# Row groups' small VectorE operations on one column each, and GpSimd's byte operations in eight pieces of 256 columns

## The chip, the cores and the metric

The kernel runs on one core of a Trainium2 chip. The metric is the device time of one execution in microseconds (us).

## The reference

Two batches of 1024 tokens with 2048 features go through a quantized product and then through a dense layer with routed low-rank additions:

```
q1 = fake_quant(layernorm(x), x1_scale, x1_zp)     # clip(round(v / s + z), 0, 255), (q - z) * s
q2 = fake_quant(ctx_4096, x2_scale, x2_zp)
x  = x + q1 @ q2                                   # (2, 1024, 2048) @ (2, 2048, 2048)
y  = layernorm(x)
w  = top-2 of softmax(y @ W_router.T), normalized, over 8 experts
x  = x + y @ W_base.T + b_base + 2 * sum_e w_e * (y @ lora_A[e].T) @ lora_B[e].T
```

## The kernel before

The kernel is written engine by engine: each engine has its own program in a fixed order, and semaphores tie them together. Nothing is scheduled at run time, so the order of work on an engine is the order of its code.

Only the first product concerns us. A "row" is a tile of 128 tokens by 2048 features; there are 8 for each batch, numbered T = 0 to 15. For each row VectorE (DVE) takes statistics (`ln_stats_of`: four `bn_stats`, one `bn_aggr`, and, at the last row of a group, two small operations L950 and L951 that put variance + eps and minus the mean in the small tile `lnt`). Rows go in groups of one or two (`LN_GROUPS`: rows 0, 1, 2, 3-4, 5-6, 7, 8-9, ...). ScalarE (ACT) takes the square root (`ln_std_of`), and `ln_scale_of` on DVE makes from it, with one Newton step, a scale (column 4 of `lnt`) and an offset (column 5) for each row of the group. With these, either ACT (`ln_bytes_of`) or GpSimd (POOL, `row_bytes_of`, for rows 2, 4, 6 and 9) turns the row into bytes. TensorE (PE) turns the bytes (`turn(T)`, L1700), ACT copies them out of PSUM (`ln_copy`, L724), and they are the moving side of the first product.

The other side, the context, comes in 32 columns n of 128 x 2048 values, 1 MB each. POOL turns each to bytes (`ctx_bytes_of`, L1611), and ACT (L733) or DVE (`ctx_ready_of`, L1005) makes them float16. PE works in chunks (`chunk(n, c)`, 16 matmuls, L1721) into a ring of four PSUM banks; DVE frees a bank with `take_y(n, c)` (L1022), which adds the chunk to x. Behind it come ACT's column addition and high part (`col_add_of`, `hi_of`, L747), DVE's low part (`lo_of`, L1028) and the sum of squares (`acc_of`, L1041). SyncE (SP) issues all loads from one queue in order; a context load waits for POOL to be done with the buffer's former column.

POOL's own order is: small constants, then context bytes 0, row 2, context 1, row 4, context 2, row 6, context 3, context 4, row 9, context 5 and so on. PE's order up to the first full stretch is: `turn(0)`, `turn(1)`, `turn(2)`, `chunk(0,0)`, `turn(3)`, `turn(4)`, `chunk(1,0)`, `chunk(0,1)`, `chunk(1,1)`, `chunk(2,0)`, `turn(5)`, `turn(6)`, `chunk(2,1)`, `chunk(0,2)`, `turn(7)`, `chunk(1,2)`, `chunk(2,2)`, with short sums between them.

Of the kernel before, what the change touches and what calls it, by code (L numbers as in the profile page):

```python
# [8 lines left out]
ALU = mybir.AluOpType  # L9
# [9 lines left out]
CH = 512  # L19
# [83 lines left out]
def xattn_ffn(nc, x, xT, ctx, s1, z1, s2, z2, w_t, w_n, bias, ar, b_t, outT):  # L103

    es = ExitStack()
    with es:
# [120 lines left out]
        def pc(i):  # L227
            return par[:, i:i + 1]

        S1, Z1, S2, Z2 = pc(0), pc(1), pc(2), pc(3)  # L230
        IS1, IS2, C1, C2, D1, D2 = pc(4), pc(5), pc(6), pc(7), pc(8), pc(9)
        RC1, RC2, LO1, HI1, LO2, HI2 = pc(10), pc(11), pc(12), pc(13), pc(14), pc(15)
        S12, ND1S, ND2S, DDS, YB = pc(16), pc(17), pc(18), pc(19), pc(20)
# [694 lines left out]
        def _(dve):  # L928
            V = nc.vector

            def ln_stats_of(T):
# [17 lines left out]
                dve.wait_ge(ln_stat, 2 * T + 2)  # L949
                V.tensor_scalar(lnt[g % 2][:, 0, 0:w], mv[:, t0:t0 + w, 1], EPS, None, ALU.add)  # L950
                V.tensor_scalar(lnt[g % 2][:, 6, 0:w], mv[:, t0:t0 + w, 0], -1.0, None, ALU.mult).then_inc(ln_var, 1)  # L951

            def ln_scale_of(g):


                t0, w = LN_GROUPS[g]
                n = lnt[g % 2]
                dve.wait_ge(ln_std, g + 1)
                V.reciprocal(n[:, 1, 0:w], std1[:, t0:t0 + w]).then_inc(ln_newton, 1)
                dve.wait_ge(ln_var, g + 1)  # L960
                dve.wait_ge(ln_newton, 4 * g + 1)
                for m in range(w):
                    ins = V.scalar_tensor_tensor(n[:, 2, m:m + 1], n[:, 1, m:m + 1], n[:, 0, m:m + 1], n[:, 1, m:m + 1], ALU.mult, ALU.mult)
                ins.then_inc(ln_newton, 1)
                dve.wait_ge(ln_newton, 4 * g + 2)
                V.tensor_scalar(n[:, 2, 0:w], n[:, 2, 0:w], -0.5, 1.5, ALU.mult, ALU.add).then_inc(ln_newton, 1)
                dve.wait_ge(ln_newton, 4 * g + 3)
                V.scalar_tensor_tensor(n[:, 4, 0:w], n[:, 2, 0:w], IS1, n[:, 1, 0:w], ALU.mult, ALU.mult).then_inc(ln_newton, 1)
                dve.wait_ge(ln_newton, 4 * g + 4)
                for m in range(w):  # L970
                    ins = V.scalar_tensor_tensor(n[:, 5, m:m + 1], n[:, 4, m:m + 1], n[:, 6, m:m + 1], Z1, ALU.mult, ALU.add)
                ins.then_inc(ln_scale, 1)
# [618 lines left out]
        def _(pool):  # L1591
# [398 lines left out]
```

## Time and profile before

| | |
|---|---|
| median of 3 runs | 987.72 us (987.59 to 987.99) |
| the profiled execution | 987.62 us, span 985.9 us |
| PE busy | 958.5 us (97% of the span), 5829 matmuls |
| DVE busy | 791.3 us (80%) |
| ACT busy | 429.3 us (44%) |
| POOL busy | 150.3 us (15%), 204 instructions |
| moved by DMA | 185.65 MB |

Times in the trace are from the start of the span. The execution's own time is 1.7 us longer than its span. A busy share is a mean over stages: PE's 97% says that the 27 us in which it is not busy are what a change outside PE can reach, and the views by stage show where they lie.

### The profile page before, as it was taken

What the parts mean: (1) busy time and instruction counts of PE and PEld (TensorE: products, weight loads), DVE (VectorE), ACT (ScalarE), POOL (GpSimd) and SP (SyncE); (2) the same over time, 40 slices, a digit from 0 to 9 for tenths busy, and PEclk for the clock granted to TensorE, in tenths of its full rate; (3) what the DMA queues carried; (4) which work ended last, traced back from release to release, by engine and by line L of the source; (5) the groups of instructions that cost most, each with busy time, mean ns of one, the idle gap of its engine ahead of it and who ended that gap; (6) DMA issues with size and microseconds to landing.
All of it is one profiled execution on the core that took longest, in us unless ns stands there. A gap on an engine that the chain in (4) does not pass through costs nothing.

```text
span 985.9 us, 15054 instructions
## 1 busy us (share of the span) xinstructions
PE 958.5 (97%) x5829; PEld 525.2 (53%) x5829; DVE 791.3 (80%) x1427; ACT 429.3 (44%) x466; POOL 150.3 (15%) x204
## 2 busy tenths in 40 slices
PE   2899999999999999999999999999999999999998
PEld 1776666666799444444444444444444444444444
DVE  7998988989636878997876887757879788798786
ACT  4888887565532444554444542212232323323310
POOL 5655435455000000000000000000000000000000
PEclk9999999999999999999999999999999999999999
DMA  9977776987434337866674674178533143242220
GB/s 375 372 263 296 261 295 236 324 310 254 142 116 143 126 81 251 268 191 242 226 232 161 200 249 103 40 238 283 170 114 127 61 144 128 71 154 93 85 75 33
DMA packets 62311, 185.65 MB, mean 188 GB/s; under 512 B 6896, under 2 KB 19488, under 8 KB 56096
## 3 DMA queue, kind: packets, MB, share of 16 engines
q1 hardware_dynamic: 58648, 174.18, 49.7%
q0 software_dynamic: 1280, 2.12, 2.4%
q10 hardware_dynamic: 2312, 8.39, 2.2%
q8 instruction: 46, 0.75, 0.3%
q14 instruction: 25, 0.20, 0.1%
HBM read 151.07 MB, written 33.60 MB: 187 GB/s over the span
## 4 chain that ended last, share of the span: by engine, by line
PE 92%; DVE 0%; issue 0%
PE pair L1884 34%; PE pair L1908 29%; PE pair L1721 19%; PE pair L1846 5%; PE pair L1856 4%; PE pair L1920 1%; PE pair L1729 0%; PE pair L1700 0%; PE pair L1826 0%; PE pair L1741 0%; DVE xt L1022 0%; DVE sq L1536 0%; DVE u L1538 0%; PE pair L1735 0%; PE pair L1745 0%
## 5 line engine op out<-in xcount | busy, mean ns | idle before, releaser
L1884 PE MATMUL pair<-x2p,w_p 128*128 128x512 f16 x1536 | 337.0, 379 | 0.0
L1884 PEld LDWEIGHTS pair<-x2p,w_p 128*128 128x128 f16 x1536 | 150.3, 98 | 180.4
L1721 PE MATMUL pair<-q1T,ctx_q 128*128 128x342 f16 (+2 forms) x1584 | 228.3, 304 | 1.8 <-DVE xt L1022 1.7
L1721 PEld LDWEIGHTS pair<-q1T,ctx_q 128*128 128x128 f16 x1584 | 152.7, 97 | 72.0 <-issue 2.8
L1908 PE MATMUL pair<-x2p,w_slot 128*128 128x512 f16 x744 | 163.8, 379 | 0.0
L841 ACT ACTIVATE sq<-pair,lsc 128x512 f32<-128x512 f32 x64 | 43.5, 681 | 210.0 <-PE pair L1856 174.1
L1611 POOL TENSOR_SCALAR ctx_u<-ctx_f,par 128x512 uint8<-128x512 f32 x128 | 113.5, 901 | 96.6 <-DMA ctx_f<-in_ctx 79.7
L1908 PEld LDWEIGHTS pair<-x2p,w_slot 128*128 128x128 f16 x744 | 72.9, 98 | 87.7
L869 ACT ACTIVATE w_slot<-w_q,usc 128x1024 f16<-128x1024 f32 x32 | 36.5, 1146 | 91.9 <-DVE usc L1442 27.2
L1908 PE MATMUL pair<-x2p,x2p 128*128 128x512 f16 x336 | 74.3, 379 | 0.0
L739 ACT ACTIVATE xt<-xt,colt 128x1024 f32<-128x1024 f32 x32 | 36.7, 1146 | 54.8 <-DVE xt L1022 54.8
L1466 DVE SCALAR_TENSOR_TENSOR w_slot<-w_q,usc,w_slot 128x1024 f16<-128x1024 f32 x32 | 40.6, 1282 | 22.8 <-ACT w_slot L869 22.8
L1028 DVE SCALAR_TENSOR_TENSOR x2p<-xt,xs,x2p 128x1024 f16<-128x1024 f32 x32 | 42.4, 1327 | 17.4 <-ACT x2p L747 17.2
L1022 DVE SCALAR_TENSOR_TENSOR xt<-pair,par,xt 128x342 f32<-128x342 f32 (+2 forms) x99 | 53.9, 552 | 2.9 <-PE pair L1721 2.1
L869 ACT ACTIVATE x2p<-w_q,usc 128x1024 f16<-128x1024 f32 x24 | 27.4, 1146 | 65.9 <-DVE usc L1442 15.8
L825 ACT ACTIVATE w_p<-w_f,wsc 128x1024 f16<-128x1024 f32 x32 | 34.9, 1138 | 48.7 <-DVE wsc L1211 48.7
L1908 PEld LDWEIGHTS pair<-x2p,x2p 128*128 128x128 f16 x336 | 32.8, 98 | 39.7
L1908 PE MATMUL pair<-x2p 128*128 128x512 f16 x240 | 52.9, 379 | 0.0
L1856 PE MATMUL pair<-hwT,b_p 128*128 128x512 f16 x192 | 51.7, 379 | 0.0
L1672 POOL DMA_DIRECT2D scratch<-w_max x16 | 9.0, 559 | 279.8 <-DVE w_max L1200 261.5
L1411 DVE SCALAR_TENSOR_TENSOR u<-sq,bias_s,u 128x512 f32<-128x512 f32 x63 | 47.4, 752 | 2.2
L1846 PE MATMUL pair<-ar_p,x2p 128*128 128x137 f16 x768 | 48.3, 224 | 0.0
(217 smaller groups left out, 1110.0 us busy)
## 6 DMA issues: line engine op xcount, KB each, us to landing
ctx_f<-in_ctx SPq DMA_DIRECT2D x32, 1024.0 KB, 7.6
xt<-in_xT SPq DMA_DIRECT2D x32, 512.0 KB, 4.7
w_r<-in_w_n SPq DMA_DIRECT2D x32, 512.0 KB, 7.0
w_f<-in_w_t SPq DMA_DIRECT2D x32, 512.0 KB, 5.9
w_q<-in_w_t SPq DMA_DIRECT2D x32, 512.0 KB, 4.9
outT<-u SPq DMA_DIRECT2D x63, 256.0 KB, 3.2
rows<-in_x SPq DMA_DIRECT2D x15, 1024.0 KB, 9.7
x_kept<-xt ACTq DMA_DIRECT2D x16, 512.0 KB, 4.3
```

What stands on the lines that cost most here:

```text
L841: A.activation(sq[m % 2][:, :], lora_bank(m)[:, :], ACT.Copy, scale=by).then_inc(lora_taken, 1)
L869: A.activation(w_of(i, p, 0), w_q[s][:, :, :], ACT.Copy, scale=usc[:, i % 2, (3 if by == 4 else 2):(4 if by == 4 else 3)]).then_inc(s_hi, 1)
L1022: V.scalar_tensor_tensor(xt[n % 3][:, t], bank[at % RING][:, 0:w], S12, xt[n % 3][:, t], ALU.mult, ALU.add).then_inc(y_taken, 1)
L1028: V.scalar_tensor_tensor(x2p[b][:, j, 1, :], xt[n % 3][:, :], xs[:, b, 0:1], x2p[b][:, j, 0, :], ALU.mult, ALU.subtract).then_inc(lo_done, 1)
L1411: V.scalar_tensor_tensor(o[:, :], s[:, :], bias_s[:, j:j + 1], o[:, :], ALU.add, ALU.add).then_inc(u_ready, 1)
L1466: V.scalar_tensor_tensor(w_of(i, p, 1), w_q[s][:, :, :], usc[:, i % 2, (3 if by == 4 else 2):(4 if by == 4 else 3)], w_of(i, p, 0), ALU.mu ...
L1611: ins = G.tensor_scalar(ctx_u[n % 2][:, c], ctx_f[n % 2][:, c], IS2, Z2, ALU.mult, ALU.add)
L1721: ins = M.matmul(bank[at % RING][:, 0:w], ctx_q[n % NQ][:, k, :], q1T[b][:, k, t0:t0 + w], start=(k == 0), stop=(k == KT - 1))
L1846: ins = M.matmul(h_tile(b, t), x2p[b][:, k, xh, t * P:(t + 1) * P], ar_p[ah][:, k, :], start=(k == 0 and q == 0), stop=(k == KT - 1 and q ...
L1856: ins = M.matmul(lora_bank(m)[:, :], b_p[s][bh][:, :], hwT[b][hh][:, t], start=(q == 0), stop=(q == 2))
L1884: M.matmul(base_bank(m)[:, :], w_p[j % 2][wh][:, k, :], x2p[0][:, k, xh, t], start=(k == 0 and q == 0), stop=(k == KT - 1 and q == 2))
L1908: ins = M.matmul(product_bank(i, p)[:, :], w_of(i, p, wh)[:, k // 4, (k % 4) * P:(k % 4 + 1) * P], x_of(p, k, xh), start=(k == 0 and q == ...
```

## The change

In the row groups, each small operation that had two columns for a group of two rows becomes two operations of one column. The three kinds of `scalar_tensor_tensor`, which read two tensors of `lnt`, become `tensor_scalar` operations of one column, whose other operands are given as scalars of the partition. The algebra is reordered for it: (v r r - 3) times (-r / (2 S1)) in place of (1.5 - 0.5 v r r) times IS1 times r, so that `NIS1` takes the place of `IS1`, and a chain of four dependent steps behind the reciprocal becomes one of three. On POOL each burst of four operations of 512 columns becomes one of eight operations of 256.

```diff
-                V.tensor_scalar(lnt[g % 2][:, 0, 0:w], mv[:, t0:t0 + w, 1], EPS, None, ALU.add)
-                V.tensor_scalar(lnt[g % 2][:, 6, 0:w], mv[:, t0:t0 + w, 0], -1.0, None, ALU.mult).then_inc(ln_var, 1)
+                for m in range(w):
+                    V.tensor_scalar(lnt[g % 2][:, 0, m:m + 1], mv[:, t0 + m, 1:2], EPS, None, ALU.add)
+                for m in range(w):
+                    ins = V.tensor_scalar(lnt[g % 2][:, 6, m:m + 1], mv[:, t0 + m, 0:1], -1.0, None, ALU.mult)
+                ins.then_inc(ln_var, 1)
...
                 V.reciprocal(n[:, 1, 0:w], std1[:, t0:t0 + w]).then_inc(ln_newton, 1)
                 dve.wait_ge(ln_var, g + 1)
-                dve.wait_ge(ln_newton, 4 * g + 1)
+                dve.wait_ge(ln_newton, 3 * g + 1)
                 for m in range(w):
-                    ins = V.scalar_tensor_tensor(n[:, 2, m:m + 1], n[:, 1, m:m + 1], n[:, 0, m:m + 1], n[:, 1, m:m + 1], ALU.mult, ALU.mult)
+                    V.tensor_scalar(n[:, 2, m:m + 1], n[:, 0, m:m + 1], n[:, 1, m:m + 1], n[:, 1, m:m + 1], ALU.mult, ALU.mult)
+                for m in range(w):
+                    ins = V.tensor_scalar(n[:, 3, m:m + 1], n[:, 1, m:m + 1], NIS1, None, ALU.mult)
                 ins.then_inc(ln_newton, 1)
-                dve.wait_ge(ln_newton, 4 * g + 2)
-                V.tensor_scalar(n[:, 2, 0:w], n[:, 2, 0:w], -0.5, 1.5, ALU.mult, ALU.add).then_inc(ln_newton, 1)
-                dve.wait_ge(ln_newton, 4 * g + 3)
-                V.scalar_tensor_tensor(n[:, 4, 0:w], n[:, 2, 0:w], IS1, n[:, 1, 0:w], ALU.mult, ALU.mult).then_inc(ln_newton, 1)
-                dve.wait_ge(ln_newton, 4 * g + 4)
+                dve.wait_ge(ln_newton, 3 * g + 2)
                 for m in range(w):
-                    ins = V.scalar_tensor_tensor(n[:, 5, m:m + 1], n[:, 4, m:m + 1], n[:, 6, m:m + 1], Z1, ALU.mult, ALU.add)
+                    ins = V.tensor_scalar(n[:, 4, m:m + 1], n[:, 2, m:m + 1], 3.0, n[:, 3, m:m + 1], ALU.subtract, ALU.mult)
+                ins.then_inc(ln_newton, 1)
+                dve.wait_ge(ln_newton, 3 * g + 3)
+                for m in range(w):
+                    ins = V.tensor_scalar(n[:, 5, m:m + 1], n[:, 4, m:m + 1], n[:, 6, m:m + 1], Z1, ALU.mult, ALU.add)
                 ins.then_inc(ln_scale, 1)
...
             dve.wait_ge(par_turned, 1)
+            V.tensor_scalar(S1N, bank[0][:, 0:1], -2.0, None, ALU.mult)
             V.tensor_copy(par[:, 0:4], bank[0][:, 0:4]).then_inc(par_copied, 1)
             dve.wait_ge(par_copied, 1)
-            V.reciprocal(IS1, S1)
+            V.reciprocal(NIS1, S1N)
...
-                for q in range(4):
-                    c = slice(q * CH, (q + 1) * CH)
+                for q in range(8):
+                    c = slice(q * CH // 2, (q + 1) * CH // 2)
                     ins = G.tensor_scalar(ctx_u[n % 2][:, c], ctx_f[n % 2][:, c], IS2, Z2, ALU.mult, ALU.add)
...
-                for q in range(4):
-                    c = slice(2 * q, 2 * q + 2)
+                for q in range(8):
+                    c = slice(q, q + 1)
                     ins = G.tensor_scalar(byte[:, c, :, :], row[:, c, :, :], lnt[g % 2][:, 4, m:m + 1], lnt[g % 2][:, 5, m:m + 1], ALU.mult, ALU.add)
```

On DVE, around the group of rows 5 and 6 (`lnt_146`), the program stood so before; `xt` rows are `take_y`, the `ctx_q` row is `ctx_ready_of(2)`, and `rows_0_53` is row 7:

```order
L950 TENSOR_SCALAR lnt_146<-mv 128x2
L951 TENSOR_SCALAR lnt_146<-mv 128x2
L1022 SCALAR_TENSOR_TENSOR xt_79<-pair,par,xt_79 128x256
L959 RECIPROCAL lnt_146<-std_145 128x2
L963 SCALAR_TENSOR_TENSOR lnt_146<-lnt_146 128x1 x2
L966 TENSOR_SCALAR lnt_146<-lnt_146 128x2
L968 SCALAR_TENSOR_TENSOR lnt_146<-lnt_146,par 128x2
L971 SCALAR_TENSOR_TENSOR lnt_146<-lnt_146,par 128x1 x2
L1005 TENSOR_SCALAR ctx_q_78<-ctx_u_74,par 128x2048
L1022 SCALAR_TENSOR_TENSOR xt_80<-pair,par,xt_80 128x256
L1022 SCALAR_TENSOR_TENSOR xt_79<-pair,par,xt_79 128x256
L940 BN_STATS stats_143<-rows_0_53 128x6 x4
```

and stands so now (the line numbers are those of the changed kernel, 1 to 8 higher):

```order
L952 TENSOR_SCALAR lnt_146<-mv 128x1 x2
L954 TENSOR_SCALAR lnt_146<-mv 128x1 x2
L1029 SCALAR_TENSOR_TENSOR xt_79<-pair,par,xt_79 128x256
L964 RECIPROCAL lnt_146<-std_145 128x2
L968 TENSOR_SCALAR lnt_146<-lnt_146 128x1 x2
L970 TENSOR_SCALAR lnt_146<-lnt_146,par 128x1 x2
L974 TENSOR_SCALAR lnt_146<-lnt_146 128x1 x2
L978 TENSOR_SCALAR lnt_146<-lnt_146,par 128x1 x2
L1012 TENSOR_SCALAR ctx_q_78<-ctx_u_74,par 128x2048
L1029 SCALAR_TENSOR_TENSOR xt_80<-pair,par,xt_80 128x256
L1029 SCALAR_TENSOR_TENSOR xt_79<-pair,par,xt_79 128x256
L941 BN_STATS stats_143<-rows_0_53 128x6 x4
```

Nothing changes its place; nine small instructions of the group become thirteen, and none of them reads two tensors or has two columns any more, the reciprocal aside.

On POOL, the bursts from context column 0 to context column 3 stood so before:

```order
L1611 TENSOR_SCALAR ctx_u_74<-ctx_f_72,par 128x512 x4
L1625 TENSOR_SCALAR q1u_0_62<-rows_2_55,lnt_146 128x2x2x128 x4
L1611 TENSOR_SCALAR ctx_u_75<-ctx_f_73,par 128x512 x4
L1625 TENSOR_SCALAR q1u_0_62<-rows_4_57,lnt_147 128x2x2x128 x4
L1611 TENSOR_SCALAR ctx_u_74<-ctx_f_72,par 128x512 x4
L1625 TENSOR_SCALAR q1u_0_62<-rows_6_59,lnt_146 128x2x2x128 x4
L1611 TENSOR_SCALAR ctx_u_75<-ctx_f_73,par 128x512 x4
```

and stand so now:

```order
L1619 TENSOR_SCALAR ctx_u_74<-ctx_f_72,par 128x256 x8
L1633 TENSOR_SCALAR q1u_0_62<-rows_2_55,lnt_146 128x2x128 x8
L1619 TENSOR_SCALAR ctx_u_75<-ctx_f_73,par 128x256 x8
L1633 TENSOR_SCALAR q1u_0_62<-rows_4_57,lnt_147 128x2x128 x8
L1619 TENSOR_SCALAR ctx_u_74<-ctx_f_72,par 128x256 x8
L1633 TENSOR_SCALAR q1u_0_62<-rows_6_59,lnt_146 128x2x128 x8
L1619 TENSOR_SCALAR ctx_u_75<-ctx_f_73,par 128x256 x8
```

The order is the same, each burst has twice the instructions, and its semaphore still rises only behind the last of them.

## Rows read from the trace of the kernel before

**Rows 1.** Busy time by stage: window, its length, each engine, PEclk, DMA share, GB/s

```profile
20.00:40.00 20.00, 15.95 (x191) 13.56 (x192) 18.70 (x46) 14.81 (x10) 15.92 (x21) 1.00 1.02 418
...
60.00:80.00 20.00, 18.27 (x131) 11.97 (x129) 19.31 (x36) 17.63 (x15) 11.46 (x13) 1.00 0.81 302
...
100.00:985.90 885.90, 882.37 (x5104) 467.53 (x5101) 703.51 (x1226) 354.35 (x410) 90.59 (x113) 1.00 0.51 173
```

**Rows 2.** What PE waited for from 44 to 90 us: total, times, longest

```profile
PE pair L1721 <- DVE xt L1022: 1.7, 2, 1.0
```

**Rows 3.** Timeline, 72 to 80.7 us: start, us, instructions, idle before and releaser

```profile
73.29 0.44 DVE L950 TENSOR_SCALAR lnt<-mv 128x2 f32<-128x2 f32 x1
...
74.44 0.79 DVE L963 SCALAR_TENSOR_TENSOR lnt<-lnt 128x1 f32<-128x1 f32 x2
...
77.19 0.57 DVE L1022 SCALAR_TENSOR_TENSOR xt<-pair,par,xt 128x342 f32<-128x342 f32 x1
...
77.90 2.48 PE L1721 MATMUL pair<-q1T,ctx_q 128*128 128x342 f16 x16 [1.01 <-DVE xt L1022]
```

**Rows 4.** Timelines of ACT and of DVE, 43 to 100 us

```profile
52.66 2.10 ACT L716 ACTIVATE q1u<-rows,lnt 128x2048 uint8<-128x2048 f32 x1 [1.85 <-DVE lnt L971]
...
67.09 1.67 DVE L1028 SCALAR_TENSOR_TENSOR x2p<-xt,xs,x2p 128x1024 f16<-128x1024 f32 x1 [0.31 <-ACT x2p L747]
```

**Rows 5.** Timeline of DVE, 32.9 to 44.9 us

```profile
33.62 0.48 DVE L1022 SCALAR_TENSOR_TENSOR xt<-pair,par,xt 128x256 f32<-128x256 f32 x1 [0.50 <-DMA xt<-in_xT]
...
34.28 0.35 DVE L963 SCALAR_TENSOR_TENSOR lnt<-lnt 128x1 f32<-128x1 f32 x2
...
35.39 1.28 DVE L1005 TENSOR_SCALAR ctx_q<-ctx_u,par 128x2048 f16<-128x2048 uint8 x1
...
40.27 0.15 DVE L950 TENSOR_SCALAR lnt<-mv 128x1 f32<-128x1 f32 x1
40.34 0.14 DVE L951 TENSOR_SCALAR lnt<-mv 128x1 f32<-128x1 f32 x1
...
41.06 0.78 DVE L963 SCALAR_TENSOR_TENSOR lnt<-lnt 128x1 f32<-128x1 f32 x1
41.88 0.15 DVE L966 TENSOR_SCALAR lnt<-lnt 128x1 f32<-128x1 f32 x1
42.07 0.52 DVE L968 SCALAR_TENSOR_TENSOR lnt<-lnt,par 128x1 f32<-128x1 f32 x1
...
42.75 1.07 DVE L1022 SCALAR_TENSOR_TENSOR xt<-pair,par,xt 128x256 f32<-128x256 f32 x2
```

**Rows 6.** Timeline of POOL, 18 to 44 us

```profile
19.41 3.03 POOL L1625 TENSOR_SCALAR q1u<-rows,lnt 128x512 uint8<-128x512 f32 x4 [2.32 <-DVE lnt L971]
...
35.57 4.00 POOL L1625 TENSOR_SCALAR q1u<-rows,lnt 128x512 uint8<-128x512 f32 x4 [2.53 <-DVE lnt L971]
39.55 3.03 POOL L1611 TENSOR_SCALAR ctx_u<-ctx_f,par 128x512 uint8<-128x512 f32 x4
```

**Rows 7.** Timeline of POOL, 11 to 13.9 us, its small constants

```profile
11.23 0.29 POOL L1649 TENSOR_SCALAR par<-par 128x1 f32<-128x1 f32 x1
11.49 0.28 POOL L1650 TENSOR_SCALAR par<-par 128x1 f32<-128x1 f32 x1
```

**Rows 8.** Timeline of PE, 38 to 110 us

```profile
39.63 0.62 PE L1700 MATMUL pair<-ident,q1w 128*128 128x128 f16 x8 [0.53 <-POOL q1u L1625]
...
40.49 1.91 PE L1721 MATMUL pair<-q1T,ctx_q 128*128 128x256 f16 x16
...
46.21 0.62 PE L1700 MATMUL pair<-ident,q1w 128*128 128x128 f16 x8 [1.07 <-ACT q1u L716]
```

**Rows 9.** Timeline of DVE, 9.8 to 20 us

```profile
14.23 0.60 DVE L968 SCALAR_TENSOR_TENSOR lnt<-lnt,par 128x1 f32<-128x1 f32 x1
...
18.40 0.22 DVE L963 SCALAR_TENSOR_TENSOR lnt<-lnt 128x1 f32<-128x1 f32 x1
18.65 0.15 DVE L966 TENSOR_SCALAR lnt<-lnt 128x1 f32<-128x1 f32 x1
```

**Rows 10.** What the trace has of POOL's `ctx_u` instructions: ns min/median/max, starts

```profile
L1611 POOL TENSOR_SCALAR ctx_u<-ctx_f,par x128: 767/772/2775, 14.1 to 246.9; 128x512 uint8<-128x512 f32 x128
```

More of the change, by code:

```diff
@@ L230, in xattn_ffn @@
         S1, Z1, S2, Z2 = pc(0), pc(1), pc(2), pc(3)
-        IS1, IS2, C1, C2, D1, D2 = pc(4), pc(5), pc(6), pc(7), pc(8), pc(9)
-        RC1, RC2, LO1, HI1, LO2, HI2 = pc(10), pc(11), pc(12), pc(13), pc(14), pc(15)
+        NIS1, IS2, C1, C2, D1, D2 = pc(4), pc(5), pc(6), pc(7), pc(8), pc(9)
+        S1N, LO1, LO2 = pc(10), pc(12), pc(14)
         S12, ND1S, ND2S, DDS, YB = pc(16), pc(17), pc(18), pc(19), pc(20)
```

## The prediction

> **What bounds the kernel now.** I read the page first: PE is busy 97% of the span. Then the busy time by stage, for where the other 27 us lie [rows 1]: from 20 to 40 us PE works 15.95 us, from 60 to 80 it works 18.27, and from 100 us to the end 882.37 of 885.90. The list of waits names no wait of PE behind 90 us. So what the change can move is the moment at which PE becomes gapless, 77.90 us, and nothing later, as long as POOL's longer bursts keep up.
>
> From 44 us on PE has three waits: 1.07 us before `turn(7)` at 46.21 [rows 8], and 1.7 us in two waits for DVE to free a bank [rows 2], the last of which ends with `chunk(5,2)` at 77.90, released by DVE's take at 77.19 [rows 3]. That bounds a gain: even a DVE that is never late gives at most 1.7 + 1.1 = 2.8 us.
>
> I follow that take back. DVE is busy 19.31 of the 20 us from 60 to 80 [rows 1], with one stop, 0.31 us before the low part at 67.09, for ACT's high part [rows 4]. ACT in turn works without a stop from 52.66, when the scale of rows 8-9 lets it start that row's bytes [rows 4], having waited 1.85 us for it. So the path is: DVE's `ln_scale_of(6)` at 52.6, ACT until 67.06, DVE until 77.76, PE. Before 52.6 DVE has no stop back to 33.62, where it waits 0.50 us for the first x tile's DMA [rows 5], in a stage in which the DMA engines are full (share 1.02) [rows 1]. What DVE gains before 33.62 waits there for the same load and is lost.
>
> **The stalls.** The small operations show a price alone and a price beside POOL. A two-tensor operation of one column takes 0.22 us when POOL is idle (18.40) [rows 9], and 0.60, 0.78 and 0.52 us when a burst runs [rows 9, 5]. The 0.78 at 41.06 begins with a POOL piece (39.55 plus two pieces of 0.76), and lasts just one piece [rows 5, 6]. Between the two blocked ones stands a `tensor_scalar` of one column, 0.15 us, with POOL just as busy [rows 5]: one column and one tensor isn't blocked. The same with two columns is: L950 takes 0.44 at 73.29 [rows 3], against 0.15 for one column [rows 5].
>
> The Trainium skill (SBUF — State Buffer, The single rule) says it the same way: an exclusive lock on a port pair, held for a whole instruction, between GpSimd and VectorE operations with two SBUF inputs or in a 2-port mode. By that rule the one-column `tensor_scalar` never waits; the trace agrees with its 0.15 us.
>
> **The change part by part.**
>
> (a) DVE on the path, saved. Group of row 7: L963 0.78 and L968 0.52 fall to some 0.22 each [rows 5, 9], 0.56 + 0.30 = 0.86 us. Group of rows 10-11: L950 0.44 to 0.15, 0.29 us; L963's pair takes 0.79 [rows 3] against 0.35 for such a pair with POOL idle [rows 5], 0.44 us. In sum 0.73 us behind 67.09 and 0.86 before 42.6. The stalls before 33.62 (0.38 at 14.23 [rows 9], and others like it) are worth nothing, by the wait for the load.
>
> (b) DVE on the path, added. A dependent step costs about 0.25 us from start to start (18.40 to 18.65) [rows 9] or 0.19 (41.88 to 42.07), and an independent instruction behind another 0.07 (L950 to L951) to 0.13 (the second of a pair, 0.35 less 0.22) [rows 5]. For a group of one row one step of 0.19 goes and one of 0.1 comes: 0.1 less. For a group of two, the step with four instructions costs 0.64 in place of 0.38, the next 0.38 in place of 0.20, and one step of 0.26 goes: 0.18 more; L950 and L951 become four, 0.14 more. What a `tensor_scalar` of one column with two pointers costs is in no row; between the 0.15 of one without [rows 5] and the 0.22 of the operation that it replaces [rows 9] I take 0.22; at 0.15 it would be some 0.1 less for each group. On the path there are the groups of rows 5-6 (+0.18), 7 (-0.1), 8-9 (+0.32) and 10-11 (+0.32). The instruction `S1N` (+0.07, at 9 us) is hidden by the same load.
>
> (c) POOL. No piece of 256 columns is in the trace. From below: it costs half of a piece of 512, 0.385 us, and a burst stays 3.03. From above: it costs as much as a piece of 512, 0.77, and a burst takes 6.1. Between them I take the middle between one column with a pointer (0.29 long, 0.26 from 11.23 to the next start) [rows 7] and 512 columns (0.76 to the next) [rows 6], the two rows on either side: 0.51 us, a burst of 4.07, 1.04 more. The Trainium skill (GPSIMD Engine Reference, Elementwise — side-by-side cycle accounting) gives 1.8 cycles an element at 1.2 GHz, and predicts 768 ns for 512 elements from it with no fixed part; by it 256 would take 384 ns and nothing would be added. The row of 0.29 us for one column speaks against that.
>
> (d) What POOL's microsecond does. Before, POOL stood idle 2.32 and 2.53 us for DVE's scales ahead of rows 2 and 6 [rows 6]; the second is what takes up the longer bursts. Row 2 starts at 18.95 (19.41 less 0.38 and 0.1), and row 2, context 1, row 4 and context 2 then run on end: 18.95 + 4 x 4.07 = 35.23, where context 2 ended at 35.57 - 2.53 = 33.04 before [rows 6]. DVE wants context 2 at 35.39 + 0.18 = 35.57 [rows 5]: just in time. Row 6 starts behind it, and loses the 1.0 us that it lost before (4.00 against 3.03) to the same DVE operation of 1.28 us [rows 5, 6]: it ends at 35.57 + 0.18 + 1.0 + 4.07 = 40.8 in place of 39.57. `turn(6)` waits for it now as before (0.53 us at 39.63) [rows 8], so `chunk(2,1)` (40.49 + 1.91 = 42.40) [rows 8] ends at 42.40 + 1.25 = 43.65. DVE wants that chunk for the second of its takes at 42.75, which began near 43.2 [rows 5]. DVE itself would be there at 43.2 + 0.18 - 0.1 - 0.86 = 42.4, waits until 43.7, and is 0.5 us later than before. So the 0.86 us of the row-7 group is eaten whole.
>
> Queued behind that take are `bound`, the statistics of rows 8 and 9, and `ln_scale_of(6)`: ACT's start at 52.66 moves by 0.5 + 0.32 = 0.8 us. `turn(7)` depends on ACT's copies behind the standard deviation of row 7 and moves by 0.2. ACT's stretch keeps its length, and DVE's own work in it, which had 0.31 us to spare and meets POOL in pieces half as long, stays hidden. Of the 0.8 at 67.09, the change then takes off 0.73 (a), adds 0.32 (b), and the low part there, long at 1.67 us beside a burst [rows 4], is held on average for half a piece, 0.25 in place of 0.38: 0.13 less. The sum is 0.8 - 0.73 + 0.32 - 0.13 = +0.26 us. PE's gaps of 1.7 us [rows 2] only shift with it.
>
> (e) Later POOL bursts. A column takes PE 48 matmuls of 342 columns, about 7 us; POOL needs 3.03 of them, or 4.0 where it meets DVE, and then 5.1. The trace names no engine that waited for these instructions [rows 10]. POOL mostly waits for the context load, and the loads are started by the x tile's place in the same queue rather than by POOL. SP's queue: contexts 2, 3 and 4 are issued 1 to 2 us later, each while the DMA engines are full with what was issued ahead of them (share 1.02) [rows 1], so the bytes land as before; context 5 goes out behind context 3's burst (39.55 + 3.03 = 42.58) [rows 6], some 2.3 us later, and POOL wants it behind row 9, whose bytes wait for the scale of 52.66 [rows 4], ten microseconds on. I cost (e) at nothing; if the cover were gone, it would be up to 1 us for each column.
>
> The sum against the profiled execution is 987.62 + 0.26 = 987.88; the median of the runs is 0.1 above that execution, so 988.0 us.
>
> **The rivals.**
> - *Slower: POOL's bursts become the path.* Place: context 2 and row 6, at 35 to 41 us. From a burst b above 4.15 us, DVE's L1005 at 35.57 has to wait, and row 6 ends at about 20.15 + 5b; each 0.1 us on a burst costs 0.5. At +2 us in all, b is about 4.45, a piece 0.556 us. At 0.60 a piece it gives 987.9 + 5 x 0.73 = 991.5 or so, at the upper bound of 0.77 some 998. For it: a fixed cost could lie above the 0.26 of one column, since the byte operations have two pointers and another output type. Against it: the 0.29 at 11.23 [rows 7] is with a pointer too. Chance 0.09.
> - *Faster: the relief gets through.* If a piece costs 0.385, row 6 ends 0.1 later, the chunk is there, and DVE is 0.76 early at the second take; ACT starts 0.4 earlier, and with the 0.56 behind 67.09 the take at 77.19 comes 0.95 earlier: 986.8. This is the case in which the page's rate holds. Chance 0.13. PE's two waits of 1.7 us [rows 2] are all that it can use, unless `turn(7)` comes earlier too.
> - *The change doesn't free DVE:* a pointer operand may be held back like a tensor. No row shows a pointer with an SBUF input beside a running burst. The stalls in (a) then last half a piece less, and 67.09 on saves 0.4 rather than 0.73: +0.6, 988.3. Chance 0.05.
>
> **How the numbers follow.** The likeliest case (0.73) is the sum with a piece between 0.47 and 0.54 us: 987.6 to 988.8. A measurement tells 0.2%, about 2 us, from no change, so faster means below 985.7 and slower above 989.7. Faster takes 0.02, out of the second rival. Slower takes 0.09, nearly all of the first rival and a little of the others. The rest, 0.89, is the same. The range from 986.7 to 989.6 takes in the likeliest case, the rest of the second and third rivals, and the start of the first, and leaves out the rest of it.
>
> **What the new profile would show.** A POOL piece of 256 columns at 0.51 us; row 6's burst ending near 40.8; DVE stopped about 1.3 us before the second take of column 2, for PE; no one-column operation on `lnt` over 0.25 us; ACT's bytes of row 8 at about 53.5; PE's last gap ending near 78.2. The prediction is wrong if a piece costs over 0.55 us, or if the stop at 33.62 goes, since then DVE's early savings count.

## The result, and the profile after

The changed kernel takes 992.38 us (median of 6 runs, 990.52 to 993.58) beside 987.84 us of the kernel before (6 runs, 987.58 to 988.50): a ratio of 1.0043, 95% interval 1.0034 to 1.0053. It is 4.5 us slower, where 988.0 was forecast, with a range of 986.7 to 989.6. The profiled execution took 991.65 us, its span is 989.8 us against 985.9 before: 3.9 us more to find. Lines from the diff on have moved by 1 to 8: L1022, L1028, L1611, L1625, L1700, L1721 of before are L1029, L1035, L1619, L1633, L1708, L1729 here.

The busy time from 20 to 40 us, columns as in [rows 1] (PE, its weight loads, DVE, ACT, POOL), and then a part of that stretch in steps of 2 us:

```profile
20.00:40.00 20.00, 14.84 (x160) 12.73 (x161) 17.20 (x51) 14.70 (x10) 20.00 (x37) 0.91 1.02 417
```
```profile
30.00:32.00 2.00, 0.19 (x4) 0.10 (x3) 1.97 (x4) 2.00 (x2) 2.00 (x5) 0.95 0.99 397
32.00:34.00 2.00, 2.00 (x18) 1.89 (x19) 0.74 (x6) 1.84 (x3) 2.00 (x5) 0.50 1.07 438
34.00:36.00 2.00, 2.00 (x15) 1.58 (x13) 1.69 (x10) 1.04 (x2) 2.00 (x4) 0.70 0.97 397
```

POOL, busy for 15.92 us of the stretch from 20 to 40 before [rows 1], is busy for all 20 of it. And behind a PE that worked 0.19 us from 30 to 32 us the granted clock stands at 0.50 (of its two levels, 1.2 in place of 2.4 GHz) from 32 to 34 us, and at 0.70 in the mean from 34 to 36, a stretch in which it rises again; before, the whole stretch had 1.00 [rows 1].

POOL's timeline, against [rows 6]:

```profile
18.99 4.30 POOL L1633 TENSOR_SCALAR q1u<-rows,lnt 128x256 uint8<-128x256 f32 x8 [0.60 <-DVE lnt L978]
23.27 4.30 POOL L1619 TENSOR_SCALAR ctx_u<-ctx_f,par 128x256 uint8<-128x256 f32 x8
27.55 4.30 POOL L1633 TENSOR_SCALAR q1u<-rows,lnt 128x256 uint8<-128x256 f32 x8
31.83 4.30 POOL L1619 TENSOR_SCALAR ctx_u<-ctx_f,par 128x256 uint8<-128x256 f32 x8
36.11 5.27 POOL L1633 TENSOR_SCALAR q1u<-rows,lnt 128x256 uint8<-128x256 f32 x8
```

A burst takes 4.30 us, 1.27 more than the 3.03 of before, 8 pieces of 0.535 us from start to start. These five bursts stand end to end; of the 2.32 and 2.53 us for which POOL waited for DVE before [rows 6], 0.60 is left. Row 4's bytes (27.55) end at 31.85, 1.8 us later than before, and row 6's (36.11) at 41.38.

PE's timeline, against [rows 3, 8]:

```profile
31.91 1.03 PE L1708 MATMUL pair<-ident,q1w 128*128 128x128 f16 x8 [1.81 <-POOL q1u L1633]
33.59 2.70 PE L1729 MATMUL pair<-q1T,ctx_q 128*128 128x256 f16 x16
36.53 5.40 PE L1729 MATMUL pair<-q1T,ctx_q 128*128 128x256 f16 x48
43.07 1.91 PE L1729 MATMUL pair<-q1T,ctx_q 128*128 128x256 f16 x16
...
79.89 2.48 PE L1729 MATMUL pair<-q1T,ctx_q 128*128 128x342 f16 x16 [1.17 <-DVE xt L1029]
...
109.30 2.48 PE L1729 MATMUL pair<-q1T,ctx_q 128*128 128x342 f16 x16 [0.47 <-DVE xt L1029]
...
121.89 4.81 PE L1729 MATMUL pair<-q1T,ctx_q 128*128 128x342 f16 x32 [0.36 <-DVE xt L1029]
...
139.70 2.48 PE L1729 MATMUL pair<-q1T,ctx_q 128*128 128x342 f16 x16 [0.93 <-DVE xt L1029]
```

The 3.9 us stand here in two halves. The last early gap ends at 79.89, not 77.90 [rows 3]: 2.0. And behind 100 us, where the list of before had no wait of PE, there are three for DVE's take: 0.47 + 0.36 + 0.93 = 1.76. That leaves some 0.15. The windows show the same: from 120 to 140 us PE works 18.71 us, where it worked 19.90 before, and from 140 to 250 all of it in both.

Between those two halves, DVE and ACT, against [rows 4, 5]:

```profile
33.65 0.48 DVE L1029 SCALAR_TENSOR_TENSOR xt<-pair,par,xt 128x256 f32<-128x256 f32 x1 [1.15 <-DMA xt<-in_xT]
...
42.58 0.27 DVE L968 TENSOR_SCALAR lnt<-lnt 128x1 f32<-128x1 f32 x1
...
45.01 0.48 DVE L1029 SCALAR_TENSOR_TENSOR xt<-pair,par,xt 128x256 f32<-128x256 f32 x1 [1.09 <-PE pair L1729]
```
```profile
54.91 2.10 ACT L717 ACTIVATE q1u<-rows,lnt 128x2048 uint8<-128x2048 f32 x1 [2.30 <-DVE lnt L978]
```

DVE gains 0.65 us before 33.65 and gives it to the x tile's load (its stop is 1.15 where it was 0.50). The row-7 group is no longer held (0.27 where 0.78 stood), and the second take of column 2 then waits 1.09 us for PE. ACT starts row 8's bytes at 54.91, 2.25 us late.

What the trace has of the small operations on `lnt`, over all groups (ns, min/median/max):

```profile
L968 DVE TENSOR_SCALAR lnt<-lnt x16: 262/272/275, 9.2 to 136.5; 128x1 f32<-128x1 f32 x16
L970 DVE TENSOR_SCALAR lnt<-lnt,par x16: 202/204/206, 9.4 to 136.8; 128x1 f32<-128x1 f32 x16
L974 DVE TENSOR_SCALAR lnt<-lnt x16: 204/214/215, 9.7 to 137.2; 128x1 f32<-128x1 f32 x16
L978 DVE TENSOR_SCALAR lnt<-lnt,par x16: 262/272/275, 9.9 to 137.6; 128x1 f32<-128x1 f32 x16
```

The longest of 16 is 3 ns above the median: no one-column `tensor_scalar` is ever held, with one pointer (an operand given as one value for each partition) or two. But one with two pointers takes 0.27 us, not the 0.22 of the operation that it replaced.

### The profile page after: what moved, and what is told of

It reads as the page before. It is cut to its first block, busy times and chain, and to the rows that moved or that the text cites. A ratio compares the mean times of both kernels' runs of the same rounds, so it can differ in the third digit from the quotient of the medians.

```text
span 989.8 us, 15223 instructions
## 1 busy us (share of the span) xinstructions
PE 960.1 (97%) x5829; PEld 526.7 (53%) x5829; DVE 790.6 (80%) x1452; ACT 429.1 (43%) x466; POOL 219.0 (22%) x348
## 4 chain that ended last, share of the span: by engine, by line
PE 86%; DVE 0%; issue 0%
PE pair L1892 33%; PE pair L1916 29%; PE pair L1729 13%; PE pair L1854 5%; PE pair L1864 4%; PE pair L1928 1%; PE pair L1737 0%; PE pair L1834 0%; PE pair L1708 0%; PE pair L1749 0%; DVE sq L1544 0%; DVE xt L1029 0%; DVE u L1546 0%; PE pair L1743 0%; PE pair L1828 0%; PE pair L1841 0%
## 5 line engine op out<-in xcount | busy, mean ns | idle before, releaser
L1729 PE MATMUL pair<-q1T,ctx_q 128*128 128x342 f16 (+2 forms) x1584 | 229.6, 305 | 3.4 <-DVE xt L1029 3.4
L1729 PEld LDWEIGHTS pair<-q1T,ctx_q 128*128 128x128 f16 x1584 | 153.1, 98 | 74.3 <-issue 5.2
L1619 POOL TENSOR_SCALAR ctx_u<-ctx_f,par 128x256 uint8<-128x256 f32 x256 | 176.1, 702 | 40.9 <-DMA ctx_f<-in_ctx 30.4
L1029 DVE SCALAR_TENSOR_TENSOR xt<-pair,par,xt 128x342 f32<-128x342 f32 (+2 forms) x99 | 53.9, 551 | 5.1 <-PE pair L1729 3.5
L1035 DVE SCALAR_TENSOR_TENSOR x2p<-xt,xs,x2p 128x1024 f16<-128x1024 f32 x32 | 43.0, 1344 | 18.1 <-ACT x2p L748 17.8
L1916 PEld LDWEIGHTS pair<-x2p,x2p 128*128 128x128 f16 x336 | 32.9, 98 | 39.7
```

The lines of the kernel that those rows point to most:

```text
L1029: V.scalar_tensor_tensor(xt[n % 3][:, t], bank[at % RING][:, 0:w], S12, xt[n % 3][:, t], ALU.mult, ALU.add).then_inc(y_taken, 1)
L1035: V.scalar_tensor_tensor(x2p[b][:, j, 1, :], xt[n % 3][:, :], xs[:, b, 0:1], x2p[b][:, j, 0, :], ALU.mult, ALU.subtract).then_inc(lo_done, 1)
L1729: ins = M.matmul(bank[at % RING][:, 0:w], ctx_q[n % NQ][:, k, :], q1T[b][:, k, t0:t0 + w], start=(k == 0), stop=(k == KT - 1))
L1916: ins = M.matmul(product_bank(i, p)[:, :], w_of(i, p, wh)[:, k // 4, (k % 4) * P:(k % 4 + 1) * P], x_of(p, k, xh), start=(k == 0 and q == ...
```

## The experiments

Theory P (POOL's longer bursts make the loss) and theory G (DVE's longer groups) stood against each other first, and within P whether the loss is made early (before 45 us) or late (behind 80). No kernel leaves out work that the reference asks for; each ratio is to the kernel before, run beside it.

**One part alone.** From the kernel before, only POOL's two loops:

```
-                for q in range(4):
-                    c = slice(q * CH, (q + 1) * CH)
+                for q in range(8):
+                    c = slice(q * CH // 2, (q + 1) * CH // 2)
...
-                for q in range(4):
-                    c = slice(2 * q, 2 * q + 2)
+                for q in range(8):
+                    c = slice(q, q + 1)
```

> The kernel before with GpSimd's bursts in eight pieces of 256 columns and nothing else. Theory P (the bursts do it): bursts of 4.30 us in place of 3.03 delay row 4, row 6 and the context loads by themselves; 990 to 993 us, last early gap of PE ending 2 us or more later than 77.90, new waits of PE for VectorE behind 100 us. Theory G (the longer groups of two on VectorE do a good half): this kernel takes half of the loss or less, 988.5 to 990, and PE has no new wait behind 100 us.

Measured: 990.99 us (990.11 to 993.53, 5 runs), ratio 1.0034 [1.0022, 1.0047], +3.1. P holds for the larger part. PE waits for POOL twice before 45 us:

```profile
32.36 0.62 PE L1700 MATMUL pair<-ident,q1w 128*128 128x128 f16 x8 [1.65 <-POOL q1u L1625]
...
42.41 0.62 PE L1700 MATMUL pair<-ident,q1w 128*128 128x128 f16 x8 [1.14 <-POOL q1u L1625]
```

With the groups of before, row 6 ends at 42.35 (its burst starts at 37.08), later than the 41.38 of the changed kernel: there the groups' new form does help POOL, by 1.0 us. The last early gap ends at 80.54, and one late wait of 0.47 is left. The clock stays at 1.00 in this kernel.

The other part alone: the changed kernel with both loops back at four pieces of 512.

> The changed kernel with GpSimd's bursts back at four pieces of 512; VectorE's one-column operations stay. Theory P: no slower than before, and up to 1 us faster, since the 0.94 us of stalls at 41 to 42.6 us now reach the take of column 2: 986.8 to 988.0. Theory G: the groups of two are 0.4 us longer each, the loads of rows behind them come later, and PE gets waits behind 100 us: 989 to 990.5.

Measured: 988.60 us (988.15 to 988.96, 11 runs), ratio 1.0005 [0.9996, 1.0013]. The whole program's relief of DVE is worth nothing, or less; the loss of 0.66 us on the median isn't told from zero, since the interval holds 1. DVE and POOL around the row-7 group:

```profile
41.38 0.27 DVE L968 TENSOR_SCALAR lnt<-lnt 128x1 f32<-128x1 f32 x1
...
39.85 3.01 POOL L1619 TENSOR_SCALAR ctx_u<-ctx_f,par 128x512 uint8<-128x512 f32 x4
```
```profile
77.45 2.48 PE L1729 MATMUL pair<-q1T,ctx_q 128*128 128x342 f16 x16 [1.05 <-DVE xt L1029]
118.95 4.81 PE L1729 MATMUL pair<-q1T,ctx_q 128*128 128x342 f16 x32 [0.27 <-DVE xt L1029]
136.80 2.48 PE L1729 MATMUL pair<-q1T,ctx_q 128*128 128x342 f16 x16 [0.93 <-DVE xt L1029]
```

At 41.38 a two-pointer operation runs its plain 0.27 us inside a burst of 512-column pieces: the rival "the change doesn't free DVE" falls. PE's last early gap ends 0.45 us earlier than before, and 1.20 us of late waits take it back: 0.75 more in all, and 0.66 measured on the median.

**The clock.** The changed kernel with filler matmuls, so that PE isn't idle ahead of row 4:

```
             turn(3)
+            keep_busy(26)
             turn(4)
```

> The changed kernel with 26 filler matmuls between turn(3) and turn(4), in the 1.8 us in which PE waits for row 4's bytes and behind which its granted clock falls to 0.50. Theory C (the fall of the clock is a part of the first 2 us): chunk(1,0) takes 1.9 us again in place of 2.70, PE is about 1.5 us ahead at chunk(2,1), the second take of column 2 comes about 1 us earlier, and the time is 0.5 to 1.5 us under the changed kernel's 992.4. Rival (VectorE and ScalarE are late anyway by the bursts): the clock stays at 1.0 and the time stays within 0.3 us of the changed kernel.

Measured: 993.50 us (993.49 to 995.33, 5 runs), ratio 1.0057 [1.0044, 1.0070]; 1.1 us above the changed kernel, which neither theory had. The stretch behind row 4, and PE's waits, from `turn(6)` on:

```profile
32.00:34.00 2.00, 2.00 (x31) 1.89 (x29) 0.65 (x6) 2.00 (x3) 2.00 (x4) 1.00 1.04 426
```
```profile
41.48 0.62 PE L1708 MATMUL pair<-ident,q1w 128*128 128x128 f16 x8 [0.50 <-POOL q1u L1633]
...
79.10 2.48 PE L1729 MATMUL pair<-q1T,ctx_q 128*128 128x342 f16 x16 [0.93 <-DVE xt L1029]
106.45 2.48 PE L1729 MATMUL pair<-q1T,ctx_q 128*128 128x342 f16 x16 [0.74 <-DVE xt L1029]
109.87 2.48 PE L1729 MATMUL pair<-q1T,ctx_q 128*128 128x342 f16 x16 [0.93 <-DVE xt L1029]
123.75 4.81 PE L1729 MATMUL pair<-q1T,ctx_q 128*128 128x342 f16 x32 [1.66 <-DVE xt L1029]
141.54 0.74 PE L1729 MATMUL pair<-q1T,ctx_q 128*128 128x342 f16 x4 [0.92 <-DVE xt L1029]
```

The clock is whole again and the last early gap ends 0.8 us earlier (79.10, not 79.89). It isn't kept: the late waits grow from 1.76 to 4.25 us. So undoing the fall of the clock doesn't bring the time back, and an earlier start into the late stage buys nothing here. What the fall costs by itself isn't shown, since this kernel's late part differs too. One thing the first line adds: with a whole clock PE waits for row 6's bytes at `turn(6)` again, 0.50 us, though row 4's are as late as ever, and `chunk(2,1)` starts at 42.34.

**Late bursts in eight, early in four**, with DVE's new form:

```
+                parts = 8 if n >= 4 else 4
+                for q in range(parts):
+                    c = slice(q * D // parts, (q + 1) * D // parts)
```

(and in the rows' loop the same with `T >= TT`).

> The changed kernel with the bursts of rows 2, 4, 6 and of context columns 0 to 3 back at four pieces of 512; those of columns 4 on and of row 9 stay at eight of 256. If the first 2 us (PE's last early gap ends at 79.9 in place of 77.9) come from the early bursts alone and the other 2 us (waits of PE from 109 to 140 us) from the late ones: 989.5 to 990.5, gap at 78, and the late waits stay. If the late waits only follow from the early lateness: 987.5 to 988.5.

Measured: 990.18 us (988.62 to 991.79, 11 runs), ratio 1.0021 [1.0012, 1.0030]. The last early gap ends at 77.54, earlier than before, and the late waits are 0.93 + 0.33 + 0.93 = 2.2 us. So there is a late loss with an undisturbed early part: 1.6 us of time, and 1.0 us of late waits, more than in the kernel with DVE's new form alone.

**Larger pieces.** From the kernel before, two pieces of 1024 columns in a burst in place of four of 512.

> The kernel before with GpSimd's bursts in two pieces of 1024 columns and nothing else. By a straight line through what was measured (0.535 us a piece of 256, 0.757 a piece of 512) a piece has a fixed 0.31 us and 0.87 us for 1000 columns: 1.20 us for 1024, a burst of 2.40 in place of 3.03. Theory P (the length of the bursts sets the time): no slower than before, 986.5 to 987.9. Rival (what counts is how long one piece holds VectorE): held operations wait up to 1.2 us, VectorE is later at the takes at 43 and 77 us, and the time is 988.5 or more.

Measured: 989.12 us (988.65 to 990.30, 11 runs), ratio 1.0012 [1.0003, 1.0021]. What the trace has of `ctx_u`, and, in the profiled execution (the slowest of the 11), two of PE's waits:

```profile
L1611 POOL TENSOR_SCALAR ctx_u<-ctx_f,par x64: 1184/1195/3062, 14.1 to 246.9; 128x1024 uint8<-128x1024 f32 x64
```
```profile
77.69 2.48 PE L1721 MATMUL pair<-q1T,ctx_q 128*128 128x342 f16 x16 [1.91 <-DVE xt L1022]
80.73 1.47 PE L1721 MATMUL pair<-q1T,ctx_q 128*128 128x342 f16 x9 [0.56 <-DVE xt L1022]
```

A burst is 2.37 us, 0.66 shorter, and the kernel is slower all the same: PE waits 4.2 us for takes from 69 to 81, where it waited 1.7 [rows 2]. What is held on DVE can now be held for most of a piece of 1.19 us (L951 takes 1.03 us at 76.05, 0.15 before). But DVE also stops 1.74 us for an x tile's load at 64.52, which it didn't before, and no run separates the two. Of the three sizes of a piece tried, 512 columns is the best.

**DVE's new form in part**, with POOL at four pieces of 512. First only the groups of one row (the condition chooses the old form):

```
+            def FORM(g):
+                w = LN_GROUPS[g][1]
+                return w == 2
```

> GpSimd as before (four pieces of 512). The one-column operations only in the groups of one row (rows 0, 1, 2 and 7); groups of two rows in their former form. Theory G (the longer groups of two cost what PE waits behind 100 us): the 0.94 us of stalls at row 7 are gone, nothing is added on the path, and PE has no wait behind 100 us: 986.6 to 987.6. Rival (row 7's stall is eaten by PE or ScalarE, and the late waits come from elsewhere): 987.7 to 988.8, with waits behind 100 us.

Measured: 987.68 us (987.31 to 988.07, 11 runs), ratio 0.9998 [0.9989, 1.0007]. ACT's row 8 starts at 51.93, 0.73 us earlier. DVE's timeline behind it:

```profile
56.66 0.22 DVE L1052 TENSOR_SCALAR colt<-pair,par 128x1 f32<-128x1 f32 x1 [0.80 <-PE pair L1755]
...
73.64 0.79 DVE L981 SCALAR_TENSOR_TENSOR lnt<-lnt 128x1 f32<-128x1 f32 x2
74.46 0.73 DVE L984 TENSOR_SCALAR lnt<-lnt 128x2 f32<-128x2 f32 x1
```

The relief gets as far as ACT and is lost twice: DVE waits 0.80 us for PE, and at 74 us it meets POOL's burst a piece longer: the pair L981 takes 0.79 as L963 did [rows 3], and the two-column `tensor_scalar` behind it 0.73, which had been out of the burst and took 0.17 before. The gap ends at 77.66 against 77.90, and PE has a late wait of 0.41 us at 135.81, which theory G did not have.

Then the new form for rows 0 to 9, the old one (`return g >= 7`) for rows 10 to 15:

> GpSimd as before (four pieces of 512). The one-column operations in the groups of rows 0 to 9; the three last groups of two (rows 10 to 15) in their former form. Theory G: the late waits of 0.27 and 0.93 us go, the early gap ends near 77.6 since those groups keep their stalls at 73 to 75 us: 987.2 to 988.0. Rival (the late waits come from the phase of the loads, not from the groups there): they stay, 988.6.

Measured: 988.19 us (987.70 to 989.46, 11 runs), ratio 1.0003 [0.9994, 1.0011]. One late wait of 0.57 at 136.31 in place of 0.27 + 0.93, and the early gap ends at 77.98: the result lies between the two cases.

**Early bursts in eight, late in four**, with the DVE of before (`parts = 4 if n >= 4 else 8`, and `T >= TT`):

> The kernel before with eight pieces of 256 only in the bursts of rows 2, 4, 6 and of context columns 0 to 3; the later ones at four of 512. If the loss of the bursts alone (3.05 us) is made before 45 us, where POOL runs its bursts end to end: 990 to 991, the gap at 80.5 as with eight pieces throughout. If the held VectorE operations between 50 and 80 us make it: 988 to 989, the gap under 79.

Measured: 990.39 us (989.81 to 993.55, 6 runs), ratio 1.0030 [1.0018, 1.0041]. The seven bursts that begin before 43 us alone cost 2.5 us of the 4.5: the gap ends at 80.71. Which of the bursts? Only the rows' in eight:

> The kernel before with eight pieces of 256 only in the three bursts of rows 2, 4 and 6 (3.8 us more POOL work before 45 us). Theory Q (POOL runs end to end, so the added microseconds of all bursts up to context 2 and row 6 add up): about half of the loss of the early bursts, 988.8 to 989.6, and row 4's bytes end some 1.2 us later, not 2.2. Rival (only the row bursts count, PE waits for nothing else): the whole loss, 990 to 990.8.

Measured: 989.18 us (988.47 to 990.74, 11 runs), ratio 1.0013 [1.0004, 1.0021]. Row 4's bytes end at 31.74, 1.7 us later than before and not 1.2, and the gap ends at 78.78. Only the contexts' in eight:

> The kernel before with eight pieces of 256 only in the four bursts of context columns 0 to 3. Theory Q: about the other half, 988.5 to 989.6, since context 1 stands ahead of row 4 and context 2 ahead of row 6 on POOL. Rival (only the row bursts count): 987.7 to 988.2.

Measured: 987.92 us (987.38 to 988.68, 11 runs), ratio 0.9995 [0.9986, 1.0004]. POOL's timeline in that kernel, and then in the one with both:

```profile
26.80 3.04 POOL L1626 TENSOR_SCALAR q1u<-rows,lnt 128x512 uint8<-128x512 f32 x4 [0.49 <-DVE lnt L971]
29.82 4.33 POOL L1612 TENSOR_SCALAR ctx_u<-ctx_f,par 128x256 uint8<-128x256 f32 x8
35.67 4.00 POOL L1626 TENSOR_SCALAR q1u<-rows,lnt 128x512 uint8<-128x512 f32 x4 [1.52 <-DVE lnt L971]
```
```profile
27.99 4.31 POOL L1627 TENSOR_SCALAR q1u<-rows,lnt 128x256 uint8<-128x256 f32 x8 [0.23 <-DVE lnt L971]
32.27 4.31 POOL L1612 TENSOR_SCALAR ctx_u<-ctx_f,par 128x256 uint8<-128x256 f32 x8
37.07 5.28 POOL L1627 TENSOR_SCALAR q1u<-rows,lnt 128x256 uint8<-128x256 f32 x8 [0.49 <-DVE lnt L971]
```

Contexts alone cost -0.2, rows alone +1.0, both +2.5. The parts don't add, so theory Q falls: a context's 1.27 us is taken from the time in which POOL waits for DVE (1.52 us of it is left), and a row's is on the path of `turn(4)` at once. With both, POOL still waits for DVE, 0.23 and 0.49 us, but for a DVE that is late itself. Its small operations for rows 5 and 6 now run beside context 2's burst: the pair L963 takes 0.74 us at 35.01 and L966 0.51 us at 35.79. In the kernel with only the rows' in eight they take 0.35 and 0.17 us, and row 6's burst starts at 35.86, not at 37.07. So the old form of the groups and the long bursts make each other's loss larger here. PE then waits 1.15 us for row 6 and `chunk(2,1)` starts at 43.26, with a clock that stays at 1.00.

**Late bursts alone in eight**, DVE as before:

> The kernel before with eight pieces of 256 only from context column 4 and row 9 on. If the late bursts cost by themselves (the two kernels with new VectorE groups had 0.7 to 1.0 us more of late waits with them): 988.4 to 989.2. If they cost only together with the longer groups on VectorE: 987.7 to 988.2.

Measured: 989.13 us (988.42 to 991.19, 11 runs), ratio 1.0011 [1.0003, 1.0020], +1.0; two late waits of 0.57 (at 107.95) and 0.56 (at 137.53).

**A combination** of what seemed useful, groups of one row new and early bursts of 2 x 1024:

> A try at a faster kernel: one-column operations only in the groups of one row, and POOL's bursts of rows 2, 4, 6 and context columns 0 to 3 in two pieces of 1024 (2.38 us), the later ones in four of 512. Row 6's bytes end some 0.6 us earlier, so that the take of column 2 can use what VectorE gains at row 7: 986.5 to 987.5 if POOL's end is what ate that gain; 987.5 to 988.0 if ScalarE's copies or the late waits eat it anyway.

Measured: 987.83 us (987.14 to 988.57, 11 runs), ratio 0.9996 [0.9987, 1.0005]. No gain that can be told. Not every late wait asks for a changed late part: this kernel, the one with new groups of one row, and the three with early bursts alone in eight have the late part of before, and each has one wait of 0.41 to 0.57 us between 135 and 140 us.

**What makes the late half?** Three kernels from the changed one. Groups of rows 10 to 15 in the old form:

> The changed kernel with the three last groups of two rows (rows 10 to 15) in their former form, bursts of eight pieces throughout. If the longer groups make the late waits: they fall from 1.8 us to about 0.6, the time to 991.0 to 991.8. If the bursts make them: they stay above 1.4, and the time at 992 to 993.

Measured: 992.70 us (990.68 to 994.00, 5 runs), ratio 1.0045 [1.0032, 1.0058]; late waits 0.78 + 0.57 + 0.57, as foreseen for the bursts. Late bursts in four again:

> The changed kernel with the bursts from context column 4 and row 9 on back at four pieces of 512. If the late bursts make the late waits: 0.3 us of them or less, and 990.5 to 991. If the groups make them: 1.2 us stay, as with the new groups alone, and the time is 991.2 to 992.

Measured: 991.34 us (990.38 to 992.19, 5 runs), ratio 1.0032 [1.0020, 1.0045]; late waits 0.36 + 0.93, as foreseen for the groups. Both late bursts in four and the fillers:

> As the run before, with the 26 filler matmuls ahead of turn(4). If the 4.3 us of late waits of the filled kernel come from its late bursts: they fall to 1.2 us or less, the early gap stays at 79.1, and the time is 990 to 990.8, under the kernel without fillers. If the fillers or the early phase make them: over 2 us stay, and the time is 992 or more.

Measured: 992.62 us (991.95 to 993.33, 5 runs), ratio 1.0046 [1.0032, 1.0059]; the clock at 1.00, the early gap ends at 79.65, late waits 0.93 + 1.07 + 0.93. With long bursts early, taking away either late suspect alone brings 1.0 us at most, and the fillers again make the late waits longer.

## Why the prediction was wrong

**What held.** The frame: before 90 us the last early gap of PE decides, and DVE's take releases it. One-column `tensor_scalar` isn't held beside a burst, with pointers either. DVE's early savings are lost at the x tile's load (33.65). Context 4's load goes out 3.1 us later (36.16, 33.07 before), and POOL starts on it at 46.26 as at 46.23 before. The relief of the row-7 group is eaten at the second take of column 2, which waits for PE.

**(c), a piece of 256 columns, mis-sized.** 0.51 us was taken; it is 0.535, a burst of 4.30 and not 4.07. The rival "slower" said that DVE's L1005 has to wait from a burst of 4.15 on, and gave it 0.09; at 4.30 it does wait, 0.30 us. But 0.535 lies within the 0.47 to 0.54 us of the likeliest case, and by that rival's own price, 0.5 us for each 0.1 us of burst, 4.30 gives some 988.7. The size of the piece alone doesn't lead to 992.4, and neither sign of being wrong (a piece over 0.55 us, no stop at 33.62) came true.

**(d), the step that failed first.** It followed POOL's longer bursts to PE only at context 2 and row 6, and took what PE does before them as given: row 6 at 40.8, `chunk(2,1)` ending 43.65. Row 6 was off by only 0.6 (41.38). But row 4's bytes, one burst ahead of context 2 in the same queue, moved as well: PE's `turn(4)` had already waited 0.38 us for them in the kernel before, until 30.09, and by my own sum its burst would now end at 18.95 + 3 x 4.07 = 31.16; I never set the two beside each other. The two rows, in the kernel before:

```profile
27.00 3.03 POOL L1625 TENSOR_SCALAR q1u<-rows,lnt 128x512 uint8<-128x512 f32 x4 [1.55 <-DVE lnt L971]
```
```profile
30.09 0.62 PE L1700 MATMUL pair<-ident,q1w 128*128 128x128 f16 x8 [0.38 <-POOL q1u L1625]
```

The 1.55 us ahead of row 4 are a third wait of POOL for DVE, which (d) left out. Now PE waits 1.81 us there; its clock then falls to 0.50, 16 matmuls of 256 columns take 2.70 us in place of 1.91, the 48 behind them start at 36.53 and not at 33.25 as before, and `chunk(2,1)` starts at 43.07 (before: 40.49; by (d): 41.74). Of the 1.3 us by which (d) was short, 0.6 are row 6's own lateness, since with fillers, where row 6 is the last that PE waits for, the chunk starts at 42.34; the other 0.7 come from row 4 together with the fall of the clock behind it. So the second take is at 45.01, not at 43.7; row 8 on ACT at 54.91, not 53.5; the gap ends at 79.89, not 78.2. With a whole clock the gap ends 0.8 us earlier, but that gain is not in the kernel's time. The kernels with one half of the early bursts in eight (-0.2 and +1.0 alone, +2.5 together) show that neither kind of burst makes the early loss by itself.

**(b), mis-sized.** A group of two with DVE otherwise free takes, from its reciprocal to the next operation, 1.74 us (105.66 to 107.40) against 1.37 before (102.84 to 104.21): 0.37 more, where 0.18 was forecast, mostly since each two-pointer instruction is 0.05 longer. L950 and L951 in four cost 0.10 more, forecast 0.14. A group of one takes 1.14 (42.31 to 43.45).

**(e), costed at nothing: the other half.** The prediction said that behind 90 us nothing can move, since PE has no wait there. No wait doesn't mean slack. Behind the group of rows 14-15 PE had no wait before, and now it waits 0.93 us. Late bursts in eight alone cost 1.0 us, DVE's new form alone 0.7 (an interval that holds zero), early bursts in eight alone 2.5; in sum 4.2, of 4.5 measured. That the sum fits so well is partly luck: early and late bursts alone add up to 3.5, and together they cost 3.1. In the late stage DVE stops for rows that have not landed. ACT's bytes, SP's issues and DVE's stop, after:

```profile
92.86 2.08 ACT L717 ACTIVATE q1u<-rows,lnt 128x2048 uint8<-128x2048 f32 x1
...
92.88 0.33 SPq L475 DMA_DIRECT2D ctx_f<-in_ctx  x1
94.97 0.33 SPq L470 DMA_DIRECT2D rows<-in_x  x1
...
102.02 2.47 DVE L941 BATCH_NORM_STATS2 stats<-rows 128x6 f32<-128x512 f32 x4 [0.48 <-DMA rows<-in_x]
```

The same issues were at 89.87 and 92.74 before, and DVE had no stop for those rows. The issue at 94.97 isn't held by POOL: SP issues it when ACT has read the row that had the buffer (92.86 + 2.08), and ACT is 2.2 us later than before (90.63), of which 2.0 are the early half. What is new is the flight: 7.0 us from issue to landing, 6.4 before, and 7.9 with late bursts alone in eight. SP does wait more for POOL ahead of its context loads (2.0 us from 85 to 112 us, 0.3 before), so that the context's load goes out 2.1 us ahead of the rows', not 2.9; that this lengthens the flight is not shown.

DVE's stops for rows behind 90 us and PE's late waits grow together. With the old form they are 2.7 and 0 us (before) and 3.3 and 0.6 (early bursts in eight), 3.6 and 1.1 (late bursts in eight); with the new one 2.6 and 1.2 (bursts in four), 3.1 and 1.8 (the changed kernel), 4.1 and 2.2 (late bursts in eight) and 5.0 and 4.25 (with fillers). I read that as two causes of the late part, later rows and, on top, the longer groups; it is argued from traces, and no run moved the rows' load alone.

**What stays open.** Why the kernels with fillers, whose early part is 0.8 and 1.3 us ahead, have 2.5 and 1.6 us more of late waits; and why the changed kernel's runs spread over 3.1 us, where those of before stay within 0.9. Neither is settled. On the second the traces have a hint: the changed kernel and the one with late bursts in four have the same program up to 45 us, and ACT's square root for row 1 is at 12.95 in one and at 13.46 in the other, its bytes of row 8 at 54.91 and 56.29. Half a microsecond at the start has grown to 1.4 by 55 us.

**The rivals.** "The relief gets through" needed a piece of 0.385 us. The Trainium skill (GPSIMD Engine Reference, Elementwise — side-by-side cycle accounting) leads to that, as an estimate from its best case of 1.8 cycles an element, with no fixed part in the sum; the measured 0.535 decides against it here. The Trainium skill (SBUF — State Buffer, Who interferes with whom) has no contention for a VectorE operation with at most one SBUF input outside the 2-port modes. The traces agree with it, for one column with two pointers too: 0.27 us ahead of the first burst (13.55) and in one (42.58).

## What to carry to other kernels

When a queue of bursts has slack in it, a longer burst can be free until the slack is gone, and then it moves the bursts behind it and what waits for them: walk each burst in turn against the moment at which its consumer is ready, not only the last. An engine with no wait in a stage isn't an engine with slack; ask of the producer ahead of it by how much it is in time, and of the loads that it needs when they land. To shorten what is held beside a burst, price the fixed cost of a smaller piece first: here shorter pieces and longer ones both lost.

## What the runs showed of the hardware

- A POOL `tensor_scalar` from float32 to uint8 with two pointers, from start to start: 0.535 us for 256 columns, 0.753 for 512, 1.18 for 1024. The three lie near 0.31 us fixed and 0.87 us for 1000 columns, so eight small pieces cost 1.27 us more than four.
- A one-column DVE `tensor_scalar` with two pointers takes 0.27 us, with one pointer 0.20 to 0.21, with constants 0.15, and was never held by POOL (16 of each line, the longest 3 ns above the median). A two-column one was held: 0.73 us beside a burst.
- After a wait of 1.81 us, in which PE worked 0.19 us from 30 to 32, the granted clock was 0.50 from 32 to 34 us and 0.70 in the mean from 34 to 36, and 16 matmuls took 2.70 us in place of 1.91. With fillers in that gap it stayed at 1.00. It also stayed at 1.00 where POOL's bursts alone were in eight, behind a wait of 1.65 us (0.62 us of work from 30 to 32), and where only the early rows' were, behind one of 1.65 us too (0.35 us of work).
